# Where the row maxima are subtracted in layer 2's grouped attention: VectorE or GpSimd

## The reference

```
scores = jnp.einsum('bhqd,bhkd->bhqk', q, k) / math.sqrt(HEAD_DIM)
scores = scores + bias[None]
scores = jnp.where(causal[None, None], scores, -jnp.inf)
attn = jax.nn.softmax(scores, axis=-1)
out = jnp.einsum('bhqk,bhkd->bhqd', attn, v)
out = out.transpose(0, 2, 1, 3).reshape(B, S, Q_DIM)
return out @ W_out
```

## Time and profile before

| what | value |
|---|---|
| median of 3 runs | 1352.45 us |
| the profiled execution's own time | 1352.87 us |
| its span | 1351.2 us |
| TensorE (PE) busy | 1086.0 us, 80% of the span |
| VectorE (DVE) busy | 844.4 us, 62% |
| ScalarE (ACT) busy | 605.4 us, 45% |
| GpSimd (POOL) busy | 248.3 us, 18% |
| L2_attn, from its first to its last mask operation on VectorE | 678.8 to 922.4 us |
| mean granted TensorE clock | 0.90 of full speed |

### The profile page before, as it was taken

How to read it: one execution, slowest core, us unless ns; L and a number is a source line. 1 busy time by engine, 2 the same in 40 slices (tenths; PEclk the granted TensorE clock), 3 DMA queues, 4 the chain that set the end, 5 groups by cost and what they waited for, 6 DMA issues and landing times. The chain is left out here.

```text
span 1351.2 us, 22274 instructions
## 1 busy us (share of the span) xinstructions
PE 1086.0 (80%) x8547; PEld 839.1 (62%) x8547; DVE 844.4 (62%) x1959; ACT 605.4 (45%) x1204; POOL 248.3 (18%) x346
## 2 busy tenths in 40 slices
PE   6267776989998677879989988997679951867998
PEld 4234454568983465769867766775358840545997
DVE  4889985864255568542377757787666667864222
ACT  1178883755437447434344434443012213742443
POOL 2264533830001235110000000002310030111000
PEclk9688988999999779979999999999779985986999
DMA  7000000021000000200110000003000000000000
GB/s 237 19 1 1 1 1 1 2 82 44 1 1 1 1 2 1 95 0 1 53 54 1 1 1 0 1 2 125 1 1 1 1 1 0 1 1 1 1 1 16
DMA packets 10953, 25.67 MB, mean 19 GB/s; under 512 B 4104, under 2 KB 8832, under 8 KB 9568
## 3 DMA queue, kind: packets, MB, share of 16 engines
q1 hardware_dynamic: 10848, 24.24, 5.1%
HBM read 23.71 MB, written 0.52 MB: 18 GB/s over the span
## 5 line engine op out<-in xcount | busy, mean ns | idle before, releaser
L1236 ACT ACTIVATE arena<-bank,w_L_ffn_b1T 128x512 f32<-128x512 f32 x192 | 129.6, 689 | 161.4 <-PE bank L1178 161.0
L1273 DVE SCALAR_TENSOR_TENSOR x<-bank,gate_c,x 128x128 f32<-128x128 f32 x192 | 54.1, 344 | 179.3 <-PE bank L1213 175.0
L263 POOL TENSOR_TENSOR norm_rstd<-norm_std,minus_half 128x4 f32<-128x4 f32 x24 | 25.1, 1046 | 645.3 <-DVE norm_std L258 645.3
L1178 PE MATMUL bank<-x_high,w_low 128*128 128x512 f32 x264 | 111.7, 423 | 18.7 <-DVE w_low L1187 17.7
L1213 PEld LDWEIGHTS bank<-bufA,arena 128*128 128x128 f32 x1024 | 120.4, 194 | 2.3
L1213 PE MATMUL bank<-bufA,arena 128*128 128x128 f32 x1024 | 121.2, 277 | 0.0
L1178 PE MATMUL bank<-x_low,w_high 128*128 128x512 f32 x264 | 105.8, 401 | 0.0
L1178 PE MATMUL bank<-x_high,w_high 128*128 128x512 f32 x264 | 105.8, 401 | 0.0
L494 ACT ACTIVATE arena<-arena 128x128 f32<-128x128 f32 x256 | 80.4, 395 | 42.8 <-DVE arena L502 42.8
L2133 ACT ACTIVATE arena<-arena 128x512 f32<-128x512 f32 x64 | 40.3, 630 | 122.9 <-DVE arena L2182 122.9
L1178 PEld LDWEIGHTS bank<-x_high,w_low 128*128 128x128 f32 x264 | 51.5, 195 | 28.5 <-DVE w_low L1187 12.6
(11 more groups left out here) (437 smaller groups left out, 2452.7 us busy)
## 6 DMA issues: line engine op xcount, KB each, us to landing
bufA<-in_L_ffn_w SPq DMA_DIRECT2D x4, 2048.0 KB, 10.2
bufB<-in_L_ffn_W SPq DMA_DIRECT2D x2, 2048.0 KB, 10.2
bufB<-in_L_ffn_Wgu SPq DMA_DIRECT2D x1, 2304.0 KB, 8.5
bufA<-in_L_attn_Wqkv SPq DMA_DIRECT2D x1, 2048.0 KB, 7.8
bufB<-in_L_ffn_Wd SPq DMA_DIRECT2D x1, 1152.0 KB, 10.8
arena<-in_L_attn_Wout SPq DMA_DIRECT2D x1, 1024.0 KB, 9.9
x<-in_x SPq DMA_DIRECT2D x1, 512.0 KB, 3.6
ctxT<-in_ctxT SPq DMA_DIRECT2D x1, 512.0 KB, 4.0
```

The source lines that it names most:

```text
L263: pool.tensor_tensor(rstd[:, c], std[:, c], mhalf[:, c], ALU.pow).then_inc(norm[st]["rstd"].sem, 1)
L1178: m = pe.matmul(bank[:, :], a[:, ws], b[:, c], start=n == 0, stop=n == 2)
L1236: act.activation(m["h"][k % 2][:, f, :], banks[f][:, :], ACT.Gelu, bias=b1[:, c:c + 1]).then_inc(g["hidden"].sem, 1)
L1273: dve.scalar_tensor_tensor(x_blk(4 * t + j), banks[4 + n % 4][:, j * P:(j + 1) * P], gc[:, 4 * t + j, u:u + 1], x_blk(4 * t + j), ALU.mult ...
```

## The change

The subtraction leaves VectorE's program. The maxima now count up "peak"; GpSimd waits for it, subtracts in place, and counts up "lowered", for which ScalarE waits as before.

```diff
-            ("v_edge", 1), ("scored", 2 * UNITS), ("masked", 2 * UNITS), ("lowered", 2 * UNITS), ("exped", 2 * UNITS),
+            ("v_edge", 1), ("scored", 2 * UNITS), ("masked", 2 * UNITS), ("peak", 2 * UNITS), ("lowered", 2 * UNITS), ("exped", 2 * UNITS),
@@ layer2_attention_pool
             rstd_pool(pool, "L2_attn", 1)
+            for n in range(2 * UNITS):
+                t3 = b2["a"][n % 4].rearrange("p (j t) -> p j t", t=P)
+                pool.wait_ge(*b2g["peak"](n + 1))
+                pool.tensor_tensor(t3, t3, bc(b2["mx"][n % 8], 2, P), ALU.subtract).then_inc(b2g["lowered"].sem, 1)
@@ layer2_attention_dve
                     dve.wait_ge(*g["masked"](U0 + k + 1))
-                    dve.tensor_reduce(mx, t3, AX.X, ALU.max).then_inc(*dve_step.next())
-                    dve.wait_ge(*dve_step.now())
-                    dve.tensor_tensor(t3, t3, bc(mx, 2, P), ALU.subtract).then_inc(g["lowered"].sem, 1)
+                    dve.tensor_reduce(mx, t3, AX.X, ALU.max).then_inc(g["peak"].sem, 1)
```

## The result

The changed kernel took **1366.35 us** (median of 4 runs, 1362.05 to 1367.4) against 1352.63 for the kernel before on the same chip (4 runs, 1351.9 to 1353.19): ratio 1.0096, interval 1.0073 to 1.0118, 13.7 us slower. The forecast was 1364.5 with a range of 1360 to 1369. The profiled execution took 1366.99 us with a span of 1365.2 and a mean granted TensorE clock of 0.901; before, the span was 1351.2 and the clock 0.903.

The account below looks back on a forecast made before the run. The prediction took the pair's chain through VectorE's even subtraction, ScalarE's exponential and copy, and TensorE's wait as the bound. Thirty pairs at 0.40 us add 12.0 to 1352.45, other terms zero: 1364.5 us, range 1360 to 1369.

Parts of the forecast that it names:

- The link: Even unit, start of maxima to start of exponential: 1.44 us before, 1.84 after, so +0.40 us per paying pair.
- a dearer GpSimd: Rival: even subtractions on GpSimd take 1.54 or 1.27 us, giving 1379.5 or 1371.4 us; chance 0.08.
- Thirty pairs: Pairs of units in the changed stage that pay the longer link: 15 a half, 30 x 0.40 = 12.0 us.
- 24 + 6 waits: TensorE waits for ScalarE's copies: 24 pairs with projection parts, plus three paying last-group pairs in each half.
- The fourth pair of the last group: Leads to the half's end: odd mask up to 0.4 us sooner, odd link 0.40 longer, so zero.
- The odd unit's subtraction: Moved to GpSimd, its exponential starts 0.40 us later, but about 2 us of slack remain: zero.
- VectorE's relief: VectorE loses 64 subtractions, 44 us busy time: counted zero. As the faster rival: 8.7 us less, 1343.8; chance 0.03.
- GpSimd's queue: Two subtractions make 2.1 us in 7.9, over 3 us apart, so none waits for another: no cost.
- the lower clock: Rival: four more 10 us stretches at 0.83 TensorE clock add 6.8 us, giving 1371; chance 0.06.
- the high end of its range: All 32 pairs at 0.40 plus two stretches of lower clock, 12.8 + 3.4 us: 1368.7 us.
- a link of the chain: Even unit's subtraction, before ScalarE's exponential and copies, lies on the chain setting the pair's period of 7.54 us.
- TensorE's slack in the chain: TensorE's wait for ScalarE's copy before the next projection part, in pairs with projections: 0.37 us.

Follow-up runs that it names:

- the split: Changed kernel with each tile's subtraction divided, VectorE taking two heads and GpSimd the other two, ScalarE waiting for both: 1364.53 us.
- the even unit alone: Kernel before with only the even units' subtraction moved to GpSimd, the odd ones staying on VectorE: 1366.63 us, ratio 1.0108.
- the doubled subtraction: Changed kernel with an extra GpSimd subtraction of zeros ahead of the real one: odd units only 1369.70 us, even units only 1434.96 us.
- the repeat: The changed kernel measured once more, nothing altered: 1366.86 us against 1353.58 for the kernel before, ratio 1.0103.
- the three reordered kernels: ScalarE's copies before the exponential: kernel before, 1333.00 us; changed kernel, 1332.86 us; changed kernel with only the projection part's copy moved, 1337.54 us.

## Why the prediction was right

**The link.** Costed at +0.40 (0.35 of work, 0.05 of crossings) from the twin in the earlier trace rows. Measured 1.84 - 1.44 = 0.40, with the operation at 1041 ns 64 times. Correct to the hundredth; the twin had the same shape, operands and neighbours. The rival "a dearer GpSimd" falls with it: the 1.54 us of the earlier trace rows appeared in none of the 64. SBUF — State Buffer, "Who interferes with whom", of the Trainium skill names VectorE instructions with two SBUF inputs, or in a two-port mode, as those that contend. By that rule, with the mask reading a bank, 1.04 was to be expected, and the trace agrees. GPSIMD Engine Reference, "Elementwise — side-by-side cycle accounting", of the Trainium skill gives the factor 1.96, for rows of 2048 elements; by it the loss would have been 21 us, an estimate. The trace has 1.51 at 512 elements a row, and the split shows 0.85 to 0.42, a factor of 2.0, at 256: the factor depends on the size, and the row of the same shape was the one to use.

**Thirty pairs.** The step from 24 + 6 waits to 30 pairs at 0.40 is shown by the pairs themselves and by the even unit alone, which has the whole loss. The fourth pair of the last group was costed at zero. At the first end the wait for the even unit grew from 1.01 to 1.41 us and the one for the odd unit fell from 0.48 to nothing; at the second end the second went from 0.38 to nothing. The reason held too: alone, the longer odd link costs 0.3 to 0.4 us there, and the odd mask, which starts 0.35 us sooner after the even one (2.26 against 2.61), takes it back.

**The zeros.** The odd unit's subtraction at zero is shown (1.0006, every pair but the first of the second half unchanged). Of its slack of about 2 us the doubled subtraction used 1.5 without harm in the pairs with projections. VectorE's relief, 41.6 us of busy time off (44 forecast), bought nothing in the pairs: with the even subtractions alone moved, or all of them, they are the same 7.93, and the formula with the link leaves nothing over for it. GpSimd's queue never held a subtraction up: in front of all 64 it was idle and waited for VectorE.

**What the sum lacked.** 30 x 0.39 is 11.7 us; measured were 13.7, and 13.3 in the repeat. The prediction had the lower clock as a rival of four more stretches, 6.8 us at 0.06, and as two in the high end of its range; and it named more stretches of lower clock in 677 to 930 as a sign of being wrong. That sign came, with four slices against two, though for less than the rival's price. One place is explained, which the argument had passed over: the stage's first pair, where TensorE already waited 2.32 us, and with 0.39 more the full grant was lost, for 1.0 us. It is shown for that pair by giving it back to VectorE. Some 1 to 1.5 us more lie where no instruction changed (0.5 before the stage, 0.9 behind it). Stretches of lower clock fall differently in each execution, as the second half's first pair shows with 7.78 and 8.70 us in two runs of the same kernel. Whether those 1.4 us belong to the change or to the execution profiled was not settled. The central 1364.5 was 1.9 us low, and that the total fell inside the range rests on the 3.4 us that its high end had for such stretches without saying where: all 32 pairs alone would end at 1365.3.

**The cause behind the number.** The prediction called the even subtraction a link of the chain. The experiments narrow this: it is a link only because ready copies stand behind the exponential in ScalarE's order. With two of them in front, the subtraction may be on either engine and a pair with projections is 6.90 us, TensorE being full; in the last group the copy of the turned tile keeps it a link (6.01 against 6.41). The prediction also gave TensorE's slack in the chain as 0.37 us; taking the stop away brought 0.63. No term of its sum used that number, but the forecasts of the three reordered kernels did, and were 4 to 8 us too high. The reordered version is the best measured here, 1333 us with either engine, 1.5% faster than the kernel before.

## What to carry to other kernels

An idle engine and a loaded one say nothing about what a move is worth: find the engine whose waits set the period, see which instruction it waits for, and look at what that instruction stands behind in its own queue. If a ready piece of work is queued behind a wait for something late, additions to the late chain are paid in full, and reordering that queue can be worth more than a shift of work between engines (here 20 us against -13.7). Count a stop of TensorE as the distance between the starts on both sides of it, not as the idle time shown. When the moved operation has a twin in the same trace, with the same shape and neighbours, price the whole link from it, crossings included, and leave rules of thumb aside.

## What was not expected of the hardware

- **Longer waits of TensorE went with a lower clock, but not one to one.** With 0.76 us of wait in a pair of 7.93 the grant stayed 1.00; with 1.88 us in a pair of 9.05 it fell to 0.83 or near it in many slices of 10 us, and a cost of 33 us became 68.6. In the stage's first pair a wait of 2.32 us kept the grant in three traces of three, and about 2.7 us lost it in four of four. But pairs with the same 1.88 us came out at 9.05 and at 10.7, and in the second half 2.32 us did not keep the clock: the length of the wait alone does not decide it, and no run here separates what else does.
- **GpSimd's time is far from proportional to the columns**: 1.04 us for 128x512, 0.85 for 128x256, while VectorE went from 0.69 to 0.42. Splitting the tile between the two by columns therefore made the link longer than with VectorE alone, 1.71 us against 1.44.
- **A second wait in front of an activation can move its table load**: with one wait (the kernel before) the load of the exponential's table ran at 677.53 us, while ScalarE would have waited anyway; with two (the divided tile) it ran at 682.20, behind them, and 1.28 us moved from a hidden place onto the path.
